# The first batch's chain: the bias row made earlier, VectorE by halves, identity products in TensorE's idle stretches

## The chip, the cores and the metric

The kernel runs on one core of a Trainium2 chip. The metric is device time in microseconds (us) for one launch of the whole program, here the median over runs. Before the change it is 997.85 us over 3 runs (994.13 to 998.16).

## What is computed

Two transformer layers over 8 sequences of 256 tokens, 256 features, in f32. Only the first attention matters here: every step that the change touches belongs to it, or to the bias table of the second attention that is built meanwhile.

```python
proj = x @ w_qkv                       # 2048 x 768
q, k, v = split(proj)                  # 16 heads of 16
q, k = apply_rope(q, cos, sin), apply_rope(k, cos, sin)
q = layernorm(q, ln_scale, ln_bias)    # over the 16 of a head
k = layernorm(k, ln_scale, ln_bias)
a = tril((q @ k.T) ** 4)
out = (a / sum(a)) @ v @ w_out
...
rel = clip(pos[None] - pos[:, None] + 63, 0, 126)
scores = scores + rel_pos[rel].mean(-1)    # second attention's bias
```

## The kernel before

Each engine has its program written out by hand, in order, and waits on semaphores. The layers are phases. Phase 0 and 1 (first attention and its feed-forward) run together over 8 batches of 256 tokens, each batch as 8 slots (two heads per slot); then comes the second attention, then the experts. f32 accuracy is kept by splitting an operand in a high and a low part and making three products (lines 445, 446 and 447, one helper).

Ahead of slot 0 of batch 0 stands a start that nothing overlaps with, and the change is in it alone. Its steps before the change:

- TensorE (PE): `x_turn(0, 0)` turns x (line 641). `qk(0, 0, t)`, six products of 512 columns for each token half t, waits for the first attention's weights. Between the two halves stands the product of line 870, which lays the means of the relative table out as a row; it waits for `rel_step`, counted by VectorE. Then `v(0, 0)` (12 products of 256 columns), `x_turn(0, 1)`, and the product of line 879, which mirrors the skewed bias and waits for two loads. Then `qk(0, 1, 0..1)` for batch 1, and `heads(0, 0, 0..1)` (line 676), which turn the first heads of batch 0 and wait for `split_ready`. Then the slots.
- VectorE (DVE): low parts of x and of the weights (lines 1694, 1754, 1954), the sum over the relative table and its scale (lines 1757 and 1759), then batch 0's chain: rotation of each token half (`rope_half`, lines 1786 to 1789, three operations), with the three copies of the bias row between them (`diagonal`, lines 1766 to 1768), rotated sum, sum per head, centring, scale, variance, reciprocal, normalising and bias over all 1024 columns at once (lines 1794 to 1823), the copy of the mirrored bias (line 1967) and eight low parts of the heads (line 1833). After them `rope_half(1, t)` of batch 1, and slot 0's fourth power (line 1842), which waits for GpSimd's masks.
- ScalarE (ACT): high parts, the square of the centred values (line 1286), the deviation (1291), eight high parts of heads (1302), the copies of turned heads (1247, 1307), then the squares of scores (1332).
- SyncE (SP): loads of x, weights, tables and the relative table (line 482), the first six tiles of the feed-forward's weights (line 487), then it waits for `diag_ready`, stores the bias row to memory (line 505), waits for it and loads it skewed (line 509).

Batch 0's `in_step` runs to 13, as each later batch's does.

## Time and profile before

| | |
|---|---|
| median of 3 runs | 997.85 us (994.13 to 998.16) |
| the profiled execution | 999.12 us, its span 997.1 us |
| PE busy | 882.9 us, 89% |
| DVE busy | 704.8 us, 71% |
| ACT busy | 693.2 us, 70% |
| POOL busy | 260.6 us, 26% |
| mean granted TensorE clock | 0.967 |

A row of the timeline has the start in us from the span's start, the time from the first to the last instruction that it merges, engine, line, operation, output and inputs, and in brackets the idle time of the engine ahead of it with what ended it. A matmul's duration is longer than the distance to the next, since they are pipelined: the price of one in a row of many is the distance between starts.

### The profile page before, as it was taken

The page shows a single profiled execution, that of the slowest core. Times are in us where ns is not written, and L with a number is a line of the kernel's source. Part 1 is how long each engine was busy: PE and PEld are TensorE (multiplying, and loading weights), DVE is VectorE, ACT ScalarE, POOL GpSimd, SP SyncE. Part 2 cuts the span into 40 slices and gives each one's busy share as a digit, 9 for nine tenths or more (in the row PEclk, how much of TensorE's full clock was granted, in tenths as well). Part 3 has the DMA queues.
Part 4 walks back from the last instruction along what each step waited for, and adds up shares of the span by engine and source line. Part 5 has one row for each costly group of instructions (what it writes and reads, how often), then busy time and mean ns, then how long its engine had stood idle before and what let it go on. Part 6 is the DMA issues. An engine that isn't in the chain of part 4 may idle for free.

```text
span 997.1 us, 21097 instructions
## 1 busy us (share of the span) xinstructions
PE 882.9 (89%) x7200; PEld 719.8 (72%) x7200; DVE 704.8 (71%) x2130; ACT 693.2 (70%) x1538; POOL 260.6 (26%) x360
## 2 busy tenths in 40 slices
PE   4778899999899988888989898989888999899995
PEld 3556788888788975666666666666665888789884
DVE  6877788888855567778787778787777562365437
ACT  2878766867765358988888888888888322366646
POOL 0345622333432202002020102010100347334432
PEclk9989999999999989999999999999999999999997
DMA  6203022010000102011111111101020312244434
GB/s 191 65 1 107 5 72 86 12 33 23 22 23 23 43 12 65 2 26 42 26 40 27 38 30 33 34 10 46 9 62 23 101 55 94 70 112 113 113 129 183
DMA packets 54761, 54.87 MB, mean 55 GB/s; under 512 B 17953, under 2 KB 48929, under 8 KB 54658
## 3 DMA queue, kind: packets, MB, share of 16 engines
q1 hardware_dynamic: 51250, 44.18, 15.1%
q0 software_dynamic: 3408, 9.34, 2.8%
q8 instruction: 61, 1.00, 0.4%
q14 instruction: 42, 0.34, 0.1%
HBM read 32.85 MB, written 20.65 MB: 54 GB/s over the span
## 4 chain that ended last, share of the span: by engine, by line
PE 53%; DVE 18%; ACT 16%; issue 8%; DMA 2%; POOL 1%; another core or an unknown queue 1%; DVEq 0%; ACTq 0%; SPq 0%; POOLq 0%
PE ps L445 11%; PE ps L447 10%; PE ps L446 10%; PE ps L968 5%; PE ps L985 4%; ACT G L1487 4%; PE ps L676 3%; PE ps L956 3%; ACT wu_rows L1487 3%; ACT G L1497 2%; DVE G L2032 2%; PE ps L749 2%; PE ps L1154 1%; ACT RT L1247 1%; DVE wu_rows L2032 1%
## 5 line engine op out<-in xcount | busy, mean ns | idle before, releaser
L1487 ACT ACTIVATE G<-G,small 128x256 f32<-128x256 f32 x296 | 133.3, 511 | 25.2 <-DVE small L2032 25.0
L2032 DVE CUSTOM_DVE_ANT_0 G<-ps,nb 128x256 f32<-128x256 f32 x296 | 111.2, 420 | 44.1 <-PE ps L956 43.7
L445 PE MATMUL ps<-WU 128*128 128x256 f32 x384 | 117.0, 305 | 17.1 <-DVE wu_rows L1854 6.9
L1497 ACT COPY G<-ps 128x512 f32<-128x512 f32 x192 | 112.1, 584 | 13.9 <-PE ps L968 13.5
L2393 POOL TENSOR_SCALAR_AFFINE_SELECT G<-G 128x256 f32<-128x256 f32 x128 | 76.4, 620 | 146.5 <-ACT G L1332 146.3
L446 PE MATMUL ps<-WU 128*128 128x256 f32 x384 | 108.4, 282 | 0.0
L447 PE MATMUL ps<-WU 128*128 128x256 f32 x384 | 108.3, 282 | 0.0
L1487 ACT ACTIVATE wu_rows<-wu_rows,small 128x256 f32<-128x256 f32 x216 | 97.7, 510 | 15.2 <-DVE small L2032 14.9
L2032 DVE CUSTOM_DVE_ANT_0 wu_rows<-ps,nb 128x256 f32<-128x256 f32 x216 | 81.3, 420 | 32.4 <-PE ps L956 32.1
L968 PE MATMUL ps<-ident,G 128*128 128x128 f32 x592 | 91.8, 283 | 13.3 <-DVE G L2042 9.5
L2360 POOL TENSOR_SCALAR small<-small 128x2 f32<-128x2 f32 x16 | 7.0, 440 | 324.6 <-DVE small L1678 324.6
L445 PEld LDWEIGHTS ps<-WU 128*128 128x128 f32 x384 | 72.8, 189 | 25.5 <-issue 9.3
L968 PEld LDWEIGHTS ps<-ident,G 128*128 128x128 f32 x592 | 65.8, 142 | 26.8 <-issue 8.2
L676 PE MATMUL ps<-ident,RT 128*128 128x128 f32 x512 | 72.3, 288 | 10.6 <-ACT RT L1247 7.3
L1332 ACT ACTIVATE G<-ps 128x768 f32<-128x768 f32 x64 | 52.3, 818 | 36.8 <-PE ps L732 32.9
L968 PE MATMUL ps<-ident,wu_rows 128*128 128x128 f32 x432 | 66.8, 282 | 10.3 <-DVE G L2042 9.1
L446 PEld LDWEIGHTS ps<-WU 128*128 128x128 f32 x384 | 73.2, 191 | 0.4
L956 PE MATMUL ps<-RT 32*128 32x256 f32 x512 | 64.7, 330 | 9.9 <-DVE small L2032 8.9
L985 PE MATMUL ps<-G 128*32 128x256 f32 x1024 | 68.5, 385 | 5.1 <-ACT G L1261 4.4
L447 PEld LDWEIGHTS ps<-WU 128*128 128x128 f32 x384 | 73.0, 190 | 0.0
L676 PEld LDWEIGHTS ps<-ident,RT 128*128 128x128 f32 x512 | 60.0, 147 | 17.9 <-ACT RT L1247 10.1
L956 PEld LDWEIGHTS ps<-RT 32*128 32x128 f32 x512 | 38.5, 184 | 46.6 <-issue 33.9
(251 smaller groups left out, 2374.4 us busy)
## 6 DMA issues: line engine op xcount, KB each, us to landing
xs<-G SPq DMA_DIRECT2D x8, 645.0 KB, 6.7
G<-xs SPq DMA_DIRECT2D x39, 128.0 KB
G<-x SPq DMA_DIRECT2D x17, 256.0 KB, 2.9
G<-in_x SPq DMA_DIRECT2D x16, 256.0 KB, 2.9
wu_rows<-yy SPq DMA_DIRECT2D x8, 512.0 KB, 6.9
x<-G SPq DMA_DIRECT2D x15, 256.0 KB, 2.2
wu_rows<-in_wu SPq DMA_DIRECT2D x8, 384.0 KB, 5.1
wraw<-in_wu SPq DMA_DIRECT2D x8, 256.0 KB, 3.0
```

The costliest lines, as they stand in the source:

```text
L445: pe.matmul(o, lh, rh, start=start, stop=False, skip_group_check=True)
L446: pe.matmul(o, lh, rl, start=False, stop=False, skip_group_check=True)
L447: return pe.matmul(o, ll, rh, start=False, stop=stop, skip_group_check=True)
L676: m = pe.transpose(ps[:, bank, S * g + P * t:S * g + P * (t + 1)], w[:, t, 2 * n + g, :], ident[:])
L956: m = pe.matmul(ps[:, SCORE_BANKS[n % 3], S * t:S * (t + 1)], QT[r, g, P * t:P * (t + 1)], KTT[r, g, :], start=True, stop=True, tile_posit ...
L968: m = pe.transpose(ps[:, 2 + h % 2, S * kt + P * t:S * kt + P * (t + 1)], prob(H2 * i + h)[:, t, P * kt:P * (kt + 1)], ident[:])
L985: m = pe.matmul(ps[32 * j:32 * j + 32, MIX_BANK, S * (quad % 2):S * (quad % 2 + 1)], vp[:, kt, at:at + 32], probT(h)[:, kt, :], start=kt = ...
L1332: act.square(U(p), ps[:, b:b + 2, 0:384]).then_inc(squared, 1)
L1487: m = act.activation(p, p, ACT.Exp, scale=-1.0, bias=mneg[:, k:k + 1])
L1497: act.copy(probT(h), halves(2 + h % 2)).then_inc(probT_act, 1)
L2032: m = dve.tensor_tensor_reduce(prob(H2 * i + h)[:, t, :], ps[:, SCORE_BANKS[h % 3], S * t:S * (t + 1)], nbv[:, t, :], 1.0, -FMIN, ALU.add, ...
L2393: m = pool.affine_select(out=u, in_=u, compare_op=ALU.is_ge, fill=0.0, base=0, pattern=[[0, 2], [1, P]], channel_multiplier=-1)
```

## The change

In `first_layer` of three engines, ahead of the slots:

- PE: the product that makes the bias row stands ahead of `qk(0, 0, 0)`. `keep_busy(n)` makes n plain f32 products of the identity with itself, 128 columns, in a bank that nothing reads then: 8 after the bias row's product, 30 after `x_turn(0, 1)`, 12 after the mirroring product and, after a wait for the first batch's variance (`in_step` 14), 6 more: 56 in all.
- VectorE: the sum over the relative table and its scale stand ahead of the weights' low parts, so the wait for that load does too. The three copies of the bias row are gone from it. Each token half is rotated, summed and centred by itself; scale, variance and reciprocal stay whole; normalising and bias go by halves of the heads, each followed by its four low parts, with the copy of the mirrored bias in the first half.
- ScalarE: makes the three copies of the bias row, after the weights' high parts; the centred squares go by token halves; the high parts of each half of the heads wait for that half alone.

Batch 0 now has 19 steps in `in_step`, and `in_at(b, s)` finds a batch's step. The later batches' work is unchanged.

```diff
@@ -862,21 +867,31 @@
+                def keep_busy(times):
+                    for _ in range(times):
+                        pe.matmul(ps[:, MIX0, 0:P], ident[:], ident[:], start=True, stop=True)
                 x_turn(0, 0)
+                pe.wait_ge(rel_step, 2)
+                pe.matmul(ps[0:1, 0, 0:TABLE], small[0:TABLE, 16:17], ident[0:TABLE, 0:TABLE],
+                          start=True, stop=True).then_inc(diag_row, 1)
+                keep_busy(8)
                 pe.wait_ge(xt_ready[0], 1)
                 pe.wait_ge(aw0_ready, 2)
                 qk(0, 0, 0)
-                pe.wait_ge(rel_step, 2)
-                pe.matmul(ps[0:1, 0, 0:TABLE], small[0:TABLE, 16:17], ident[0:TABLE, 0:TABLE],
-                          start=True, stop=True).then_inc(diag_row, 1)
                 qk(0, 0, 1)
                 pe.wait_ge(aw0_ready, 3)
                 v(0, 0)
                 x_turn(0, 1)
+                keep_busy(30)
                 pe.wait_ge(skewed, 32)
                 pe.wait_ge(flip_ready, 2)
                 pe.matmul(ps[:, 1, :], flip, skewed_bias, start=True, stop=True).then_inc(bias_turned, 1)
+                keep_busy(12)
+                pe.wait_ge(in_step, in_at(0, 14))
+                keep_busy(6)
                 pe.wait_ge(xt_ready[0], 2)
                 for t in range(2):
                     qk(0, 1, t)
@@ -1281,20 +1296,34 @@
+                def diagonal():
+                    act.wait_ge(diag_row, 1)
...
+                def first_squares(t):
+                    act.wait_ge(in_step, in_at(0, 6 + 6 * t))
+                    act.square(SQ[:, 512 * t:512 * (t + 1)], CEN[:, 512 * t:512 * (t + 1)]).then_inc(cen_squared, 1)
...
                 def head_hi_parts(b):
-                    act.wait_ge(in_step, IN_STEPS * b + 13)
                     for g in range(2):
+                        act.wait_ge(in_step, in_at(b, 13 if b else 17 + 2 * g))
...
+                diagonal()
                 stage_v(0, 0)
-                centred_squares(0)
+                first_squares(0)
                 x_hi(0, 1)
+                first_squares(1)
@@ -1749,25 +1780,15 @@
                 x_lo(0, 0)
-                for k in range(KT):
-                    dve.wait_ge(aw0_hi, k + 1)
-                    dve.tensor_tensor(AW[:, 1, k, 0:512], aw0_in[:, k, 0:512], AW[:, 0, k, 0:512].bitcast(F32), ALU.subtract
-                                      ).then_inc(aw0_ready, 1)
                 dve.wait_ge(rel_loaded, 16)
                 dve.tensor_reduce(small[0:TABLE, 15:16], small[0:TABLE, 0:D2], AX_X, ALU.add).then_inc(rel_step, 1)
...
+                for k in range(KT):
+                    dve.wait_ge(aw0_hi, k + 1)
...
+                def first_centred(t):
+                    of, groups = slice(512 * t, 512 * (t + 1)), slice(2 * H0 * t, 2 * H0 * (t + 1))
+                    dve.wait_ge(in_step, in_at(0, 3 + 6 * t))
+                    step(in_step, in_at(0, 4 + 6 * t), dve.tensor_tensor(ROT[:, of], ROT[:, of], ROT2[:, of], ALU.add))
+                    step(in_step, in_at(0, 5 + 6 * t), dve.tensor_reduce(hsum[:, groups], rh[:, groups], AX_X, ALU.add))
...
+                def first_normalised(g):
...
+                    step(in_step, in_at(0, 16 + 2 * g), dve.tensor_tensor(r, r, by, ALU.mult))
+                    dve.tensor_tensor(s, r, lnt[:, D0:2 * D0].unsqueeze(1).unsqueeze(1).to_broadcast(part), ALU.add).then_inc(in_step, 1)
@@ -1953,19 +2004,17 @@
-                rope_half(0, 0)
-                diagonal()
-                rope_half(0, 1)
-                rotated(0)
-                centre(0)
-                times_scale(0)
-                variance(0)
+                for t in range(2):
+                    rope_half(0, t)
+                    first_centred(t)
+                first_scaled()
                 x_lo(0, 1)
-                normalised(0)
-                plus_bias(0)
-                dve.wait_ge(bias_turned, 1)
-                dve.tensor_copy(nb[:], ps[:, 1, :]).then_inc(bias_ready, 1)
+                first_inverse()
                 for g in range(2):
+                    first_normalised(g)
+                    if g == 0:
+                        dve.wait_ge(bias_turned, 1)
+                        dve.tensor_copy(nb[:], ps[:, 1, :]).then_inc(bias_ready, 1)
                     lo_parts(0, g)
```

`first_scaled` is the scale and the variance over all 1024 columns as before, and `first_inverse` the reciprocal.

TensorE's order ahead of the first slot, before. Line 641 is `x_turn`, 870 the bias row's product, 879 the mirroring one, 676 `heads`; rows of lines 445 to 447 are the products of `qk` and `v`.

```order
L641 MATMUL ps<-ident,G 128x128 x3
L445 MATMUL ps<-AW,RT 128x512 [waits aw0_ready,xt_ready0]
...
L447 MATMUL ps<-AW,RT 128x512
L870 MATMUL ps<-ident,small 1x127 [waits rel_step]
L445 MATMUL ps<-AW,RT 128x512
...
L641 MATMUL ps<-ident,G 128x128 [waits xt_loaded0]
L641 MATMUL ps<-ident,G 128x128 x3
L879 MATMUL ps<-G 128x512 [waits flip_ready,skewed]
L445 MATMUL ps<-AW,RT 128x512 [waits xt_ready0]
...
L676 MATMUL ps<-ident,RT 128x128 [waits split_ready0]
```

And with the change (646 is `x_turn`, 877 the bias row's product, 873 an identity product, 891 the mirroring one, 681 `heads`):

```order
L646 MATMUL ps<-ident,G 128x128 x3
L877 MATMUL ps<-ident,small 1x127 [waits rel_step]
L873 MATMUL ps<-ident 128x128 x8
L450 MATMUL ps<-AW,RT 128x512 [waits aw0_ready,xt_ready0]
...
L646 MATMUL ps<-ident,G 128x128 x3
L873 MATMUL ps<-ident 128x128 x30
L891 MATMUL ps<-G 128x512 [waits flip_ready,skewed]
L873 MATMUL ps<-ident 128x128 x12
L873 MATMUL ps<-ident 128x128 [waits in_step]
L873 MATMUL ps<-ident 128x128 x5
L450 MATMUL ps<-AW,RT 128x512 [waits xt_ready0]
...
L681 MATMUL ps<-ident,RT 128x128 [waits split_ready0]
```

Ahead of the first q and k product there now stand the bias row's product, with its wait, and 8 identity products; 48 more stand between `x_turn(0, 1)` and the first `heads`, on the one queue of the engine.

VectorE's order from the low parts of x to the first low parts of the heads, with the change (1816, 1817 and 1819 are the rotated sum, the sum per head and the centring; 1839 and 1840 normalising and bias; 1884 a low part):

```order
L1725 TENSOR_TENSOR RT<-ps,RT 128x512 [waits xt_hi0]
L1784 TENSOR_REDUCE small<-small 127x1 [waits rel_loaded]
L1786 TENSOR_SCALAR small<-small 127x1 [waits rel_step]
L1790 TENSOR_TENSOR AW<-G,AW 128x512 [waits aw0_hi] x2
...
L1816 TENSOR_TENSOR G<-G 128x512 [waits in_step]
L1817 TENSOR_REDUCE small<-G 128x32 [waits in_step]
L1819 SCALAR_TENSOR_TENSOR G<-small,G 128x512 [waits in_step]
...
L1839 TENSOR_TENSOR G<-G,small 128x4x128 [waits in_step]
L1840 TENSOR_TENSOR G<-G,lnt 128x4x128 [waits in_step]
L2017 COPY nb<-ps 128x512 [waits bias_turned]
L1884 TENSOR_TENSOR RT<-G,RT 128x2x8x16 [waits split_hi0]
```

The two small operations moved ahead of the weights' low parts, three operations of 1024 columns became six of 512 and two became four, and the first low parts stand behind half of the normalising.

## Rows read from the trace of the kernel before

**Rows 1.** Timeline of TensorE, the start (start, time, engine, line, operation):

```profile
3.65 1.09 PE L641 MATMUL ps<-ident,G 128*128 128x128 f32 x4 [3.65 <-DMA G<-in_x]
8.79 0.77 PE L445 MATMUL ps<-AW,RT 128*128 128x512 f32 x1 [4.05 <-DVE AW L1754]
...
11.61 0.58 PE L870 MATMUL ps<-ident,small 127*1 127x127 f32 x2
12.13 0.80 PE L445 MATMUL ps<-AW,RT 128*128 128x512 f32 x1
...
15.82 0.60 PE L641 MATMUL ps<-ident,G 128*128 128x128 f32 x4
```

**Rows 2.** The chain that ended last, in order of time, 10 to 34 us:

```profile
10.40 0.43 PE ps L445
...
13.82 3.29 DMA ediag<-G
17.50 4.16 DMA G<-ediag
21.70 2.07 PE ps L879 x2
...
27.85 0.23 PE ps L446
28.08 0.23 PE ps L447
28.31 0.45 PE ps L676 x4
...
32.78 0.96 DVE ring L1842
```

**Rows 3.** Timeline of VectorE, the start:

```profile
8.55 0.16 DVE L1757 TENSOR_REDUCE small<-small 127x1 f32<-127x8 f32 x1
8.74 0.15 DVE L1759 TENSOR_SCALAR small<-small 127x1 f32<-127x1 f32 x1
11.72 0.69 DVE L1786 TENSOR_TENSOR G<-ps,ropet 128x512 f32<-128x512 f32 x1 [1.31 <-PE ps L447]
12.99 0.27 DVE L1766 COPY G<-ps 1x127 f32<-1x127 f32 x1
14.59 0.69 DVE L1786 TENSOR_TENSOR G<-ps,ropet 128x512 f32<-128x512 f32 x1 [0.81 <-PE ps L447]
15.98 1.22 DVE L1794 TENSOR_TENSOR G<-G 128x1024 f32<-128x1024 f32 x1
17.24 1.22 DVE L1795 TENSOR_REDUCE small<-G 128x64 f32<-128x1024 f32 x1
26.58 2.77 DVE L1833 TENSOR_TENSOR RT<-G,RT 128x256 fp32r<-128x256 f32 x8
29.39 0.69 DVE L1786 TENSOR_TENSOR G<-ps,ropet 128x512 f32<-128x512 f32 x1
32.78 0.96 DVE L1842 TENSOR_TENSOR ring<-G 128x768 f32<-128x768 f32 x1 [0.78 <-POOL G L2393]
```

**Rows 4.** Timeline of TensorE at the experts, plain f32 products of 128 columns at full clock:

```profile
809.13 0.38 PE L1122 MATMUL ps<-G,nb 128*128 128x128 f32 x2
809.35 0.39 PE L1123 MATMUL ps<-G,nb 128*128 128x128 f32 x2
```

**Rows 5.** Timeline of SyncE's queue, the loads around the relative table's:

```profile
3.90 0.30 SPq L482 DMA_DIRECT2D small<-in_rel  x1
8.93 2.01 SPq L487 DMA_DIRECT2D wu_rows<-in_wu  x4
```

**Rows 6.** The loads of x, line 475: from issue to landing:

```profile
DMA to landing us min/median/max: 2.7/2.7/2.7
```

**Rows 7.** Stretches (from:to, length, busy PE, PEld, DVE, ACT, POOL, granted clock, DMA share, GB/s):

```profile
22.00:24.00 2.00, 2.00 (x4) 0.82 (x4) 1.97 (x4) 0.35 (x1) 0.00 (x0) 0.50 0.00 0
45.00:50.00 5.00, 1.47 (x19) 0.99 (x20) 3.80 (x9) 4.28 (x11) 0.79 (x2) 0.80 0.27 72
50.00:55.00 5.00, 5.00 (x20) 4.20 (x20) 2.87 (x7) 2.74 (x5) 1.76 (x2) 0.52 0.00 0
55.00:60.00 5.00, 3.49 (x40) 2.46 (x39) 3.79 (x6) 3.33 (x6) 2.40 (x4) 1.00 0.01 3
```

More of the change, by code:

```diff
@@ L406, in raw_count, with in_at @@
             return 16 * sum(dmas(n) for n in range(load + 1))
+        def in_at(b, s):
+            return FIRST_STEPS + IN_STEPS * (b - 1) + s if b else s
         def on_act(h):
@@ new lines, in first_scaled, with first_inverse @@
+                def first_scaled():
+                    step(in_step, in_at(0, 13), dve.tensor_tensor(rh, ch, lnt[:, 0:D0].unsqueeze(1).to_broadcast(full), ALU.mult))
+                    dve.wait_ge(cen_squared, 2)
+                    dve.tensor_reduce(hvar, sh, AX_X, ALU.add).then_inc(in_step, 1)
+                def first_inverse():
+                    dve.wait_ge(head_std, 1)
+                    step(in_step, in_at(0, 15), dve.reciprocal(hrs, hrs))
+                def first_normalised(g):
+                    part = [P, 4, H0 // 2, D0]
+                    of = slice(H0 // 2 * g, H0 // 2 * (g + 1))
+                    r, s = (a.rearrange("p (n h d) -> p n h d", n=4, h=H0)[:, :, of] for a in (ROT, SQ))
+                    by = hrs.rearrange("p (n h) -> p n h", n=4)[:, :, of].unsqueeze(3).to_broadcast(part)
+                    step(in_step, in_at(0, 16 + 2 * g), dve.tensor_tensor(r, r, by, ALU.mult))
+                    dve.tensor_tensor(s, r, lnt[:, D0:2 * D0].unsqueeze(1).unsqueeze(1).to_broadcast(part), ALU.add).then_inc(in_step, 1)
```

48 lines of the change are left out of this document (26 added, 22 removed).

## The prediction

> **What bounds the kernel now.** I read the page first: TensorE is busy 89% of the span, VectorE 71%, ScalarE 70%. But the change touches the first 30 us alone, where nothing overlaps with batch 0's chain, so I went on to the timelines of the start and to the chain that ended last. A microsecond won before the first slot is worth one at the end at most, and so is one lost.
>
> TensorE has three stretches of work in the start [rows 1]. It turns x, waits 4.05 us for the weights, makes q, k and v from 8.79 on, and turns x again at 15.82. At first 512 columns take 0.43 us each; near the end of such a series it is 0.23 us [rows 2]: the first figure is the engine at 1.2 GHz, the second at 2.4 GHz. It then idles until the skewed bias has landed at 21.66 (17.50 + 4.16), makes the mirroring product and batch 1's q and k, mostly at the low clock, and starts turning the heads at 28.31 [rows 2].
>
> VectorE meanwhile runs batch 0's chain nearly without a gap: it starts when the first six products end (11.72) and ends at 29.35 (26.58 + 2.77), that is 17.6 us later [rows 3]. Half of its low parts, those which the heads wait for, are out at about 28.0, 16.3 us after 11.72. So two chains meet at 28.0 to 28.3: VectorE's low parts and TensorE's products. From the heads to the first fourth power at 32.78 are 4.47 us [rows 2], and VectorE waited 0.78 us for it, having ended batch 1's rotation at 32.0 [rows 3]. The rest of the kernel follows from there.
>
> **The part ahead of the first q and k product.** The identity products cost TensorE time, since its queue is in order. At full clock a plain f32 product of 128 columns is two matmuls, and the next starts 0.22 us later (809.13 to 809.35) [rows 4]. At half clock I take double, 0.44 us; the bias row's product, of 127 columns, took 0.52 with its neighbour's wait (11.61 to 12.13) [rows 1]. These are the two ends.
>
> When can they start? Not before the sum over the relative table. Its load is issued at 3.90 [rows 5]; its landing isn't in the trace. No earlier than 6.6, with the 2.7 us of the quickest load, that of x [rows 6]; no later than 8.55, when VectorE did the sum with no idle time before it [rows 3]. I take 8.0, nearer the row that is on this very data. The two small operations need 0.35 us (8.55 to 8.90), so TensorE starts at 8.35. Product 0.5, eight identities 8 x 0.44 = 3.5: q and k can start at 12.4. The weights' low parts, moved behind the load (8.35 + 2 x 0.65 = 9.65), are ready by then and cost nothing; without the identities they would cost 0.9.
>
> On this load the Trainium skill has a rule (DMA: Bandwidth & Descriptors, "Why a DMA increments its semaphore by 16 and not by 1"): a transfer of 127 partitions runs on a single one of the 16 DMA engines. That speaks against a quick landing, and by it I would take the late end, 8.55: the sum would be 0.5 us higher. The trace shows neither.
>
> The clock: the fast spacing came at 13.9, 5.1 us after TensorE took up work at 8.79, and in the second series at 27.6, 5.9 us after 21.70. From 8.35 the nearer value gives 13.5. So two and a half of the six products go at 0.43 and the others at 0.23, with 0.2 for the last one's end: 12.4 + 1.1 + 0.8 + 0.2 = 14.5. VectorE's chain starts at 14.5 in place of 11.72, **2.8 us late**. Ends: landing at 6.6 gives 13.0, landing at 8.55 with the clock 5.9 us later gives 15.4.
>
> **VectorE's chain.** 1024 columns are 1.22 us and 1.26 from start to start (15.98 to 17.24), 512 are 0.69, so about 0.72 in a dependent series [rows 3]. Rotation 1.35, centred half 3 x 0.72 = 2.16, and again: 7.0. Scale and variance 2.52: 9.5; low part of x and reciprocal: 10.75. First half of the heads 2 x 0.72, the bias copy 0.65, four low parts 1.4: 14.25. Second half 1.45 and 1.4: 17.1. The three copies gone from VectorE (0.8 from 12.99 on) and the idle 0.81 at 14.59 pay for halving. So it is 2.0 us shorter to the first heads (14.25 against 16.3) and 0.5 to the end. ScalarE's copies lie where it idles, its squares beside VectorE's scale, its high parts one ahead of VectorE's low ones: nothing. By this chain the heads could be turned at 28.75 and batch 1's rotation (2.7 us) ends at 34.3.
>
> **TensorE's queue behind it.** From 14.3: second q and k half 6 x 0.227 = 1.4, v 12 x 0.12 = 1.4, x turned 0.6: 17.7. Thirty identities, now at full clock, 6.6: 24.3. The skewed bias has long landed, so its wait is gone: the store of the row is issued some 2.9 us earlier (10.94 in place of 13.82, behind six weight tiles whose last issue ends at 8.93 + 2.01) [rows 2, 5], but whether it lands earlier does not matter. Mirroring product at full clock 0.9 (2.07 at half): 25.2. Twelve identities 2.6: 27.8. The variance was there at 24.0; six more 1.3: 29.1. Batch 1's q and k 12 x 0.227 = 2.7: **31.8**. The heads then stand at 31.9 in place of 28.31, 3.6 us late, and VectorE's low parts wait for TensorE, not the reverse. First fourth power: 31.9 + 4.47 = 36.4 in place of 32.78. Batch 1's rotation (34.3) is no longer what pair 1's scores wait for, so something is given back in the first slots; I take 0.4.
>
> **Sum.** 3.6 - 0.4 = +3.2 us: 999.12 becomes 1002.3. That execution lay 1.3 us above the median of the runs, so I forecast a median of **1001.0 us**. With the ends of the landing and the clock the cost is 2.0 to 4.5.
>
> About 0.5% (5.0 us, so 992.9 and 1002.8) is what a measurement of this kernel can tell from no change; the three runs alone spread over 4.0.
>
> **Rivals.**
> - *Identities are cheap (chance 0.14).* If one in a row of many costs less than 0.156 us, the 48 fit in the 7.5 us between TensorE's other work (21.3) and the low parts at 28.75. Against it are rows 4 with 0.22. Then VectorE decides: rotation ends at 34.3 in place of 32.78 for the fourth power, +1.5 us, so 999.3. The Trainium skill (TensorE: Matmul & The Clock Gate, "Back-to-back issue gap") gives about 81 ns for a matmul of 128 columns in a stream with weight loads, so 0.16 us for the two; by that it would be on the border of this case. Rows 4 show 0.11 each.
> - *The clock pays it back, not slower than before (0.20).* Right after the start, at 45 to 50, TensorE is busy 1.47 of 5 us, and then, at 50 to 55, busy all of the time at a granted 0.52, at 2.87 for VectorE [rows 7]. That low stretch is on the path. With TensorE's own idle time filled in the start and batch 1's products done ahead of slot 0, the gap at 45 may shrink enough that the clock stays up. Price: 5.0 us at half clock are 2.5 won, with the neighbouring edges 3.4. 3.2 - 3.4 = -0.2: 997.7. It decides the result if the granted clock stays at 1.00 over the 10 us from 45 on (from 48 on, with the shift). For it: TensorE without a pause in the start stays at full clock (it was 0.50 at 22 to 24 [rows 7]). Against: the work of the slots, which makes that gap, is the same.
> - *The start is wholly cold (0.16).* The table lands at 8.55 and the clock rises only behind the first q and k: the chain starts at 15.4, heads +4.5. A further low stretch of the length of the one at 50 to 55 then falls in the first slots and adds 3.4: +7.9, 1005.7.
> - *Forecast (0.50)*: 1000 to 1003.
>
> **How the numbers follow.** Faster by over 0.5% needs the second rival and a start at its early end, and 3 us more: 0.04. Slower by over 0.5% is the third rival with the upper edge of the forecast: 0.18. The rest, 0.78, is within 0.5%. The range 995.0 to 1004.5 takes in the forecast with its ends, the first rival and most of the second; a tenth is left out at each side.
>
> **What would show it.** In the changed profile: the relative table's sum at 8.0 to 8.6; the first q and k product at 12 to 13 and not at 8.8; VectorE's first rotation at 13.0 to 15.4; identity products 0.22 apart, 0.44 before the clock rises; the granted clock at 1.00 from 14 to 35; no wait ahead of the mirroring product; the first heads at 31 to 33 with TensorE busy before them, and VectorE idle some 2 us ahead of its first fourth power. I am wrong if the identities end before VectorE's low parts, or if the first fourth power comes at the old time or sooner, or if the low clock at 50 to 55 is gone.

## The result and the profile after

The changed kernel takes 1003.94 us (median of 5 runs, 1003.65 to 1006.11), the kernel before in runs beside it 996.76 (5 runs, 994.13 to 998.16). The ratio is 1.0080 [1.0062, 1.0098]: slower by 0.8%. The forecast was 1001.0; the time lies inside the range of 995.0 to 1004.5, close to its upper end, but slower by over 0.5% had been given a chance of 0.18 only. A later comparison of the same two kernels gave 1.0079 [1.0054, 1.0104].

| | before | after |
|---|---|---|
| the profiled execution | 999.12 us, span 997.1 | 1003.65 us, span 1001.6 |
| PE busy | 882.9 us | 891.4 us |
| DVE busy | 704.8 us | 705.9 us |
| ACT busy | 693.2 us | 694.5 us |
| mean granted TensorE clock | 0.967 | 0.973 |

TensorE is 8.5 us busier, in matmuls that nobody reads, and its mean clock is higher; the time is longer. Where it came from is in the first 40 us. TensorE's timeline of the changed kernel (columns as in [rows 1]):

```profile
8.85 0.58 PE L877 MATMUL ps<-ident,small 127*1 127x127 f32 x2 [4.05 <-DVE small L1786]
9.36 3.78 PE L873 MATMUL ps<-ident 128*128 128x128 f32 x16
12.79 0.77 PE L450 MATMUL ps<-AW,RT 128*128 128x512 f32 x1
...
15.04 0.39 PE L452 MATMUL ps<-AW,RT 128*128 128x512 f32 x1
15.27 0.40 PE L450 MATMUL ps<-AW,RT 128*128 128x512 f32 x1
...
18.52 6.86 PE L873 MATMUL ps<-ident 128*128 128x128 f32 x60
25.23 1.02 PE L891 MATMUL ps<-G 128*128 128x512 f32 x2
26.09 4.18 PE L873 MATMUL ps<-ident 128*128 128x128 f32 x36
30.02 0.48 PE L450 MATMUL ps<-AW,RT 128*128 128x512 f32 x1
...
32.87 1.03 PE L681 MATMUL ps<-ident,RT 128*128 128x128 f32 x8
```

The first q and k product stands at 12.79 where it was at 8.79 [rows 1]. Ahead of it are the wait for the relative table (to 8.85) and eight identity products, 3.43 us from 9.36 to 12.79. From 15.04 to 15.27 the spacing is 0.23: the clock is up from there. From 12.79 to 35 TensorE has no gap over 0.3 us: the 60 matmuls of the thirty identity products take 6.71 us, the 36 of the later eighteen 3.93, and batch 1's products and the heads wait their turn behind them. The heads start at 32.87, where they started at 28.14 by the same timeline (the chain of [rows 2], which goes by ends, has 28.31).

VectorE's timeline of the changed kernel:

```profile
8.44 0.16 DVE L1784 TENSOR_REDUCE small<-small 127x1 f32<-127x8 f32 x1 [2.30 <-DMA small<-in_rel]
...
15.47 0.69 DVE L1807 TENSOR_TENSOR G<-ps,ropet 128x512 f32<-128x512 f32 x1 [4.35 <-PE ps L452]
...
28.36 1.43 DVE L1884 TENSOR_TENSOR RT<-G,RT 128x256 fp32r<-128x256 f32 x4 [0.18 <-ACT RT L1331]
...
31.89 1.43 DVE L1884 TENSOR_TENSOR RT<-G,RT 128x256 fp32r<-128x256 f32 x4 [0.78 <-ACT RT L1331]
33.36 0.69 DVE L1807 TENSOR_TENSOR G<-ps,ropet 128x512 f32<-128x512 f32 x1
...
37.51 1.13 DVE L1893 TENSOR_TENSOR ring<-G 128x768 f32<-128x768 f32 x1 [1.53 <-POOL G L2442]
```

The table's sum is done at 8.44 after 2.30 us of waiting for the load, so it landed 4.5 us after its issue at 3.90. The chain starts at 15.47 in place of 11.72 [rows 3], its first four low parts are out at 29.8, ahead of the heads at 32.87, and the first fourth power is at 37.51 in place of 32.78: 4.7 us later. The chain of waits of the changed kernel says the same from behind (start, length, what held):

```profile
3.90 4.51 DMA small<-in_rel
8.85 0.58 PE ps L877 x2
9.43 3.71 PE ps L873 x16
...
18.69 6.70 PE ps L873 x60
...
26.25 4.02 PE ps L873 x36
...
37.51 1.13 DVE ring L1893
```

All 56 identity products stand on it, 14.4 us: what was meant to fill idle time is now on the critical path.

SyncE's queue in the changed kernel shows what the early bias row bought:

```profile
11.70 0.29 SPq L510 DMA_DIRECT2D ediag<-G  x1
17.67 0.80 SPq L514 DMA_DIRECT2D G<-ediag  x2
```

The store is issued 2.1 us earlier than at 13.82 [rows 2], but SyncE waits for it until 17.67, before until 17.11 (13.82 + 3.29). That is 6.0 us after its issue, behind the six weight tiles issued ahead of it. The Trainium skill (DMA: Bandwidth & Descriptors, "Queues, rings and completion order") has each DMA engine take the descriptors of one queue in ring order. A late store behind six tiles would fit that, but no run here takes the tiles away, so the cause is not shown.

And the stretches of the changed kernel that answer to [rows 7] (busy us of PE, PEld, DVE, ACT and POOL, granted clock, DMA share, GB/s):

```profile
22.00:24.00 2.00, 2.00 (x21) 2.00 (x20) 1.93 (x3) 0.63 (x1) 0.00 (x0) 1.00 0.18 60
45.00:50.00 5.00, 4.49 (x32) 2.84 (x28) 4.11 (x5) 3.38 (x7) 2.36 (x4) 0.66 0.81 254
50.00:55.00 5.00, 1.88 (x22) 1.12 (x22) 3.38 (x8) 4.37 (x11) 0.79 (x2) 0.75 0.26 66
55.00:60.00 5.00, 5.00 (x21) 4.28 (x22) 3.19 (x8) 2.65 (x5) 2.18 (x2) 0.56 0.00 0
```

The clock is at full speed at 22 to 24, as meant. But the low stretch of the first slots has only moved: TensorE is busy 5.00 of 5 us at a granted 0.56 from 55 on. Nothing is paid back: the fifth fourth power is at 62.51, before at 57.53, so 5.0 us late.

### The profile page after: what moved, and what is told of

It reads as the page before. It is cut to its first block, busy times and chain, and to the rows that moved or that the text cites. A ratio compares the mean times of both kernels' runs of the same rounds, so it can differ in the third digit from the quotient of the medians.

```text
span 1001.6 us, 21327 instructions
## 1 busy us (share of the span) xinstructions
PE 891.4 (89%) x7312; PEld 730.3 (73%) x7312; DVE 705.9 (70%) x2132; ACT 694.5 (69%) x1542; POOL 261.8 (26%) x360
## 4 chain that ended last, share of the span: by engine, by line
PE 56%; DVE 18%; ACT 14%; issue 8%; DMA 1%; POOL 1%; SPq 0%; DVEq 0%; ACTq 0%; POOLq 0%
PE ps L450 11%; PE ps L452 10%; PE ps L451 10%; PE ps L983 5%; PE ps L1000 5%; ACT G L1518 4%; PE ps L681 3%; PE ps L971 3%; ACT wu_rows L1518 3%; DVE G L2081 2%; ACT G L1528 2%; PE ps L873 1%; PE ps L754 1%; PE ps L1169 1%; ACT RT L1262 1%
## 5 line engine op out<-in xcount | busy, mean ns | idle before, releaser
L1518 ACT ACTIVATE G<-G,small 128x256 f32<-128x256 f32 x296 | 133.4, 511 | 26.1 <-DVE small L2081 26.0
L2081 DVE CUSTOM_DVE_ANT_0 wu_rows<-ps,nb 128x256 f32<-128x256 f32 x216 | 81.2, 419 | 31.8 <-PE ps L971 31.5
L1361 ACT ACTIVATE G<-ps 128x768 f32<-128x768 f32 x64 | 52.2, 816 | 37.3 <-PE ps L737 32.9
```

What stands on the lines that cost most here:

```text
L1361: act.square(U(p), ps[:, b:b + 2, 0:384]).then_inc(squared, 1)
L1518: m = act.activation(p, p, ACT.Exp, scale=-1.0, bias=mneg[:, k:k + 1])
L2081: m = dve.tensor_tensor_reduce(prob(H2 * i + h)[:, t, :], ps[:, SCORE_BANKS[h % 3], S * t:S * (t + 1)], nbv[:, t, :], 1.0, -FMIN, ALU.add, ...
```

## Experiments

The theory behind all of them: every identity product costs its full time on TensorE's in-order queue. The rivals: that the table's early wait is the cost, that the chain by halves is (ScalarE's part of it had been taken as nothing), or that the loss lies in later stretches of low clock. Measured milestones are put together in a table at the end of this section.

### First set: one part at a time

Kernel a, no identity products at all:

```diff
-                keep_busy(8)
-                keep_busy(30)
-                keep_busy(12)
-                pe.wait_ge(in_step, in_at(0, 14))
-                keep_busy(6)
```

> The change without any of the 56 identity products; all else as changed. Theory A (TensorE's own queue makes the delay, the identity products fill it and the start's delay goes to the end one for one): the first q and k product at 10.1, VectorE's chain starts at 12.9 (changed kernel 15.5, before 11.7), TensorE idles again ahead of the mirroring product until the skewed bias lands at about 22, heads at 28.5, first fourth power at 33.0 (changed kernel 37.5, before 32.8). Time within 1 us of before, 997. Theory R (the work by halves, the moved wait for the table or the ScalarE copies cost the time): heads stay at 31 or later, time 1001 or more. Theory C (the low clock stretches behind the start differ, and that is the loss): heads at 28.5, but the time stays over 1000.

Measured: ratio 1.0027 [1.0000, 1.0053]. Of the 0.8%, 0.5 are gone. A third seems to be left without a single identity product, but the interval reaches down to none. TensorE's timeline of this kernel:

```profile
27.82 1.03 PE L681 MATMUL ps<-ident,RT 128*128 128x128 f32 x8
30.20 1.15 PE L681 MATMUL ps<-ident,RT 128*128 128x128 f32 x8 [1.34 <-ACT RT L1258]
```

The first heads are at 27.82, within what the kernel before shows (28.1, 27.3 and 26.7 in three profiles), although the chain starts 0.9 to 2.0 us later, at 12.66. But the second pair of heads waits 1.34 us for ScalarE's copy of the first, where it waited 0.24 before, and the first fourth power comes at 33.56, later than in any of those three.

Kernel b, only the first eight taken out:

```diff
-                keep_busy(8)
```

> The change without the 8 identity products ahead of the first q and k product; the other 48 stay. Theory A: VectorE's chain starts at 12.9, but TensorE's queue sets the heads: x turned at 17.3, 30 products of 0.22 to 24.0, mirroring to 24.9, 18 more to 28.9, batch 1's q and k to 31.6. Heads at 31.6, 1.4 earlier than changed; time 1.4 us below the changed kernel, 1002.5. If VectorE's chain were the limit: heads 2.6 us earlier than changed, time 1001.3.

Measured: 1.0063 [1.0029, 1.0097], the first fourth power at 34.94, 2.6 us sooner than in the changed profile above. Of the 3.4 us of queue, 2.8 are gone from the start of the chain (12.68 in place of 15.47); the clock rises at 13.0, behind the first q and k. The time shows 1.7 us, with 3.4 us of uncertainty either way in this ratio and 1.8 in the changed kernel's: that the first eight cost time is read from the trace, not from the times.

Kernel c, only the first eight left in:

```diff
-                keep_busy(30)
-                keep_busy(12)
-                pe.wait_ge(in_step, in_at(0, 14))
-                keep_busy(6)
```

> The change with the first 8 identity products alone; the 48 behind x_turn are out. Theory A: VectorE's chain starts at 15.5 as changed, and it is the limit now: low parts at 29.8, heads at 29.8 (TensorE's products are done by 29), batch 1's rotation ends at 36.0 and the first fourth power comes at 36.0 in place of 37.5. Time 1.5 us below the changed kernel, 1002.4. So each group taken out alone gives 1.4, both together 4.5. If the 48 were hidden behind VectorE's chain: the same time as changed.

Measured: 1.0043 [1.0014, 1.0072], first fourth power at 35.79. TensorE's timeline of this kernel:

```profile
22.43 2.08 PE L890 MATMUL ps<-G 128*128 128x512 f32 x2 [4.33 <-DMA G<-ediag]
25.23 0.77 PE L450 MATMUL ps<-AW,RT 128*128 128x512 f32 x1 [0.71 <-DVE RT L1722]
...
30.48 1.46 PE L681 MATMUL ps<-ident,RT 128*128 128x128 f32 x8
```

The chain starts at 14.89 with the eight and at 12.66 without any (a), and the heads that stand at 30.48 here stand at 32.87 with the 48. So in the traces both groups cost; the intervals of the times overlap. Without the later 48 the engine idles for 4.33 us, the clock falls, and batch 1's twelve products take 5.25 us (25.23 to 30.48) where they take 2.85 at full clock (30.02 to 32.87 in the changed kernel). The filling does what it is meant to do, worth 2.4 us, and costs 48 x 0.22 = 10.6 against a wait of 4.3 to 6.5 (4.33 here, 5.10 to 6.52 in the profiles of the kernel before).

Kernel d, the kernel before with the chain by halves alone (bias row, its copies on VectorE, table sum where they were; no identity product):

```diff
-                rope_half(0, 0)
-                diagonal()
-                rope_half(0, 1)
-                rotated(0)
-                centre(0)
-                times_scale(0)
-                variance(0)
+                rope_half(0, 0)
+                diagonal()
+                first_centred(0)
+                rope_half(0, 1)
+                first_centred(1)
+                first_scaled()
```

> Before, with VectorE's chain and ScalarE's part of it by halves alone: bias row's product, its copies on VectorE and the sum over the table where they were, no identity products. Theory A: the low parts of the first heads come at 26.8 in place of 28.0, but TensorE is at the mirroring product until 21.7 and at batch 1's products, at the low clock, until 28.3 as before: heads 28.3, first fourth power at 32.8, time as before within 0.5 us (996.8). Theory R (halving costs more in fixed shares than it gives): the fourth power at 33.5 or later and the time up by 1 or more.

Measured: 1.0012 [0.9995, 1.0030]: no gain. TensorE's timeline of this kernel:

```profile
27.70 1.03 PE L681 MATMUL ps<-ident,RT 128*128 128x128 f32 x8
29.82 1.14 PE L681 MATMUL ps<-ident,RT 128*128 128x128 f32 x8 [1.09 <-ACT RT L1258]
```

The same wait again, 1.09 us. VectorE's part from the first rotation to batch 1's is 18.48 us here, and 17.67 in the kernel before [rows 3]: halving makes it longer.

### Second set: a pure delay, the table, and filling in other places

Kernel e, the kernel before with 24 identity products directly ahead of the first heads:

```diff
+                keep_busy(24)
                 heads(0, 0, 0)
```

> Before, with 24 identity products directly ahead of the first heads and nothing else: a pure delay of 24 x 0.22 = 5.3 us on TensorE's queue. Theory A (a delay of the first heads goes to the end one for one): heads at 33.4, first fourth power at 38.0, time +5.2 (996.8 to 998.6 becomes 1002 to 1004). Theory C (the clock's low stretches behind the start decide): the first fourth power 5.2 later, and the time higher by another amount, 2 to 9.

Measured: 1.0049 [1.0029, 1.0070]. TensorE's timeline of this kernel:

```profile
29.17 5.52 PE L868 MATMUL ps<-ident 128*128 128x128 f32 x48
34.52 1.04 PE L676 MATMUL ps<-ident,RT 128*128 128x128 f32 x8
```

The 24 delay the heads by 5.35 us (29.17 to 34.52); the time is longer by 4.9, with an interval of 2.9 to 7.0. A delay at this place is paid about one for one, as far as this interval tells; no later slack takes it up. (The profiled execution, 1004.23 us, is the slowest of its seven; its first fourth power, 39.16, is 7.2 us behind the mean of the kernel before, since its chain also started late, at 12.45.)

Kernel f, the changed kernel with the table's load moved up to stand behind that of x:

```diff
+            sp.dma_start(small[0:TABLE, 0:D2], rel).then_inc(rel_loaded, 16)
...
-            sp.dma_start(small[0:TABLE, 0:D2], rel).then_inc(rel_loaded, 16)
```

> The changed kernel with the load of the relative table issued right behind the load of x, ahead of the weights' two loads. Theory A (the wait for the table holds up the first q and k product, together with the 8 identities behind it): the table's sum at about 5 to 6 in place of 8.44, identities end at about 10 in place of 13, VectorE's chain starts at 11.5 to 12.5 in place of 15.5, heads at about 29.5 in place of 33.0. Time 3 to 4 us below the changed kernel, 1000. If the table's wait is nothing: time as changed, 1004.

Measured: 1.0022 [1.0002, 1.0041]. VectorE's timeline of this kernel:

```profile
6.10 0.15 DVE L1784 TENSOR_REDUCE small<-small 127x1 f32<-127x8 f32 x1
...
11.86 0.68 DVE L1807 TENSOR_TENSOR G<-ps,ropet 128x512 f32<-128x512 f32 x1
...
33.75 0.96 DVE L1893 TENSOR_TENSOR ring<-G 128x768 f32<-128x768 f32 x1 [1.39 <-POOL G L2442]
```

The sum now runs at 6.10 with no wait, and the first fourth power is 3.8 us sooner than in the changed profile above. So one line of SyncE's queue wins back most of the loss: what made the first eight dear is that they stand behind a wait that ends late. Even then the changed kernel does not reach the old start (11.86 and 33.75; 10.68 to 11.72 and 31.36 to 32.78 before). Its twelve times fall in two groups of six, 995.8 to 998.3 and 1001.4 to 1004.0, for which no cause is shown; the profiled one is of the upper, and the median lies between them.

Kernel g, halves, with the copies of the bias row on ScalarE and the bias row, table sum and weights' low parts in the old order; 8 identity products directly behind `x_turn(0, 0)`, where TensorE waits for weights, 30 behind `x_turn(0, 1)`, none later:

```diff
                 x_turn(0, 0)
-                pe.wait_ge(rel_step, 2)
-                pe.matmul(ps[0:1, 0, 0:TABLE], small[0:TABLE, 16:17], ident[0:TABLE, 0:TABLE],
-                          start=True, stop=True).then_inc(diag_row, 1)
                 keep_busy(8)
...
-                keep_busy(12)
-                pe.wait_ge(in_step, in_at(0, 14))
-                keep_busy(6)
```

> The work by halves and the bias row's copies on ScalarE as changed, but the bias row's product, the sum over the table and the weights' low parts in the order of before; 8 identity products directly behind the first x_turn, in the 4 us in which TensorE waits for the weights, and 30 behind the second x_turn, in the wait for the skewed bias; none after it. Theory A: first q and k product at 8.8 and at full clock from about 9 to 10 on, VectorE's chain starts at 10.3 to 10.8 (before 11.7); the 30 identities end at 20.7, ahead of the landing at 21.9; batch 1's products end at 25.5 at full clock; first fourth power at 30.9 (before 32.8). Time 1.9 us below before. Theory R (halves cost more than they give): fourth power at 32 or later.

Measured: 1.0027 [1.0009, 1.0045]. ScalarE's timeline of this kernel:

```profile
27.61 1.32 ACT L1328 CAST RT<-G 128x256 fp32r<-128x256 f32 x4 [2.21 <-DVE G L1837]
28.84 0.57 ACT L1259 CAST RT<-ps 128x512 fp32r<-128x512 f32 x1
...
30.26 0.58 ACT L1259 CAST RT<-ps 128x512 fp32r<-128x512 f32 x1 [0.36 <-PE ps L681]
```

Here the cause of the new wait is plain. The first heads are turned from 26.30 on, but ScalarE's copies of them (line 1259) stand in its queue behind the high parts of the second half (line 1328), which wait 2.21 us for VectorE. They run at 28.84, and the second pair of heads, which waits 2.07 us for them, at 29.46. Heads that are early on TensorE are held on ScalarE.

Kernel h, the same filling with the chain left whole, that is, the kernel before with 8 and 30 identity products and the copies of the bias row on ScalarE:

```diff
                 x_turn(0, 0)
+                keep_busy(8)
...
                 x_turn(0, 1)
+                keep_busy(30)
```

> Before, with the bias row's copies on ScalarE and the 8 and 30 identity products placed as in g_fill_halves; VectorE's chain whole, not by halves. Theory A: chain starts at 10.3 to 10.8, low parts of the first heads 15.4 later at 26.0, end of the chain 16.8 later at 27.3, batch 1's rotation ends at 30.0, heads at 26.0, first fourth power at 30.5. Time 2.2 us below before; the same as g within 0.5, since halving helps the heads and costs VectorE.

Measured: 0.9971 [0.9959, 0.9983]. TensorE's timeline of this kernel:

```profile
4.64 3.62 PE L868 MATMUL ps<-ident 128*128 128x128 f32 x16
8.41 0.76 PE L445 MATMUL ps<-AW,RT 128*128 128x512 f32 x1
...
21.90 1.12 PE L886 MATMUL ps<-G 128*128 128x512 f32 x2 [0.27 <-DMA G<-ediag]
...
26.08 1.09 PE L676 MATMUL ps<-ident,RT 128*128 128x128 f32 x8 [0.31 <-DVE RT L1841]
```

The eight end at about 8.3, and the first q and k product follows at 8.41, within what the kernel before shows (8.79, 7.74, 7.75 in three profiles); the thirty end 0.27 us ahead of the bias's landing; the heads wait for VectorE. The first fourth power is at 30.77 and, in a second profile, at 30.01. VectorE's part is 16.68 us long: 1.0 us shorter than before for the three copies that went to ScalarE, 1.2 shorter than the 17.89 by halves.

### Third set: ScalarE's order, an earlier start, a cheaper product

Kernel i, as g, with ScalarE's copies of the turned heads between the two halves of its high parts:

```diff
-                head_hi_parts(0)
                 for q in range(2):
+                    head_hi_parts(0, [q])
                     turned_heads(0, q)
```

> g_fill_halves with ScalarE's copies of the first turned heads between its high parts of the first and of the second half of the heads, in place of behind both. Theory H (the first half is out early, but the copies of the turned heads wait behind the second half's high parts on ScalarE's in-order queue, so halving can't help the heads): first copies at 26.9 in place of 28.84, second turning of heads at 28.0 in place of 29.46, first squares of scores at 29.5 to 30 in place of 31.7; VectorE's second low parts 0.4 later; the first fourth power is then set by VectorE's own chain, at 32.8 in place of 33.4. Time 0.5 below g, so 998 to 1000. Theory K (the copies are not what it waits for): squares stay at 31.7.

Measured: 1.0045 [1.0029, 1.0061]. ScalarE's timeline of this kernel:

```profile
26.53 0.59 ACT L1259 CAST RT<-ps 128x512 fp32r<-128x512 f32 x1 [2.63 <-PE ps L681]
...
27.49 1.33 ACT L1328 CAST RT<-G 128x256 fp32r<-128x256 f32 x4
...
29.68 0.84 ACT L1358 ACTIVATE G<-ps 128x768 f32<-128x768 f32 x1
33.12 0.81 ACT L1358 ACTIVATE G<-ps 128x768 f32<-128x768 f32 x1 [2.60 <-PE ps L737]
```

And VectorE's second low parts:

```profile
28.25 1.43 DVE L1881 TENSOR_TENSOR RT<-G,RT 128x256 fp32r<-128x256 f32 x4 [1.56 <-ACT RT L1328]
```

The copies run at 26.53 instead of 28.84 and the squares of pair 0 at 29.68 instead of 31.75: the place of the wait is shown. But no time is won: the first fourth power, at 32.24, still stands behind VectorE's part, and pair 1's squares wait 2.60 us. The new order has moved the wait to the other side. ScalarE's second high parts now stand behind the copies, so VectorE waits 1.56 us for them where it waited 0.78 in g, and its part is 19.28 us long (10.43 to 29.71) in place of 17.89. One in-order queue serves both VectorE and the heads, and in each of the two orders tried one of them waits.

Kernel j, as h, with four identity products more ahead of `x_turn(0, 0)`:

```diff
+                keep_busy(4)
                 x_turn(0, 0)
                 keep_busy(8)
```

> h_fill_whole with 4 more identity products ahead of the first x_turn, while x is being loaded (1.5 to 3.7). Theory A (TensorE's work before raises the clock sooner): full clock by 8 to 9 in place of 9.8, chain starts at 10.2 to 10.5 in place of 10.72, first fourth power 0.2 to 0.6 earlier; time as h_fill_whole within 0.6, so 994.5, some 3 below before. Rival: the 4 hold up the turning of x: it starts later than 3.8 and the weights' first low part is waited for no more; then up to 0.3 slower than h.

Measured: 1.0006 [0.9987, 1.0025], although this profile's first fourth power, at 29.75, is the earliest so far. A start that is some 2 us earlier is not seen in the time; the table below shows where the profiles lose it again.

Kernel k, the changed kernel with a transpose, one matmul, in place of the f32 product, which is two:

```diff
-                        pe.matmul(ps[:, MIX0, 0:P], ident[:], ident[:], start=True, stop=True)
+                        pe.transpose(ps[:, MIX0, 0:P], ident[:], ident[:])
```

> The changed kernel with each of the 56 identity products made as a transpose: one matmul in place of two, so 0.11 to 0.12 us at full clock in place of 0.22, and 0.22 in place of 0.43 at half. Theory A (the queue time of the identity products is the cost): the first eight end at 11.2 in place of 12.8, VectorE's chain starts at 14.0, the 48 end 5.3 us earlier relative to the turning of x, TensorE waits for the skewed bias or the variance, and VectorE's chain (17.9 to batch 1's rotation) sets the first fourth power at about 34.8 in place of 37.5. Time 2 to 3 us below the changed kernel. If transposes did not hold the clock up: granted clock 0.5 before 25 us and the products of batch 1 spaced 0.43, the heads at 31 or later.

Measured: 1.0029 [1.0011, 1.0046]. TensorE's timeline of this kernel:

```profile
8.86 1.97 PE L873 MATMUL ps<-ident 128*128 128x128 f32 x8
...
17.00 3.44 PE L873 MATMUL ps<-ident 128*128 128x128 f32 x30
21.58 1.12 PE L891 MATMUL ps<-G 128*128 128x512 f32 x2 [1.14 <-DMA G<-ediag]
22.54 2.13 PE L873 MATMUL ps<-ident 128*128 128x128 f32 x18
...
27.80 1.09 PE L681 MATMUL ps<-ident,RT 128*128 128x128 f32 x8 [0.37 <-DVE RT L1884]
30.96 1.60 PE L681 MATMUL ps<-ident,RT 128*128 128x128 f32 x8 [2.07 <-ACT RT L1262]
```

At half the price the products fit: the mirroring product waits for its data, the heads wait for VectorE, and 5 us of the loss are gone. This is the first rival of the prediction, made true, which gave it +1.5 us; measured are 2.9, with an interval of 1.1 to 4.6. The wait of the second heads for ScalarE, 2.07 us, is back with it: in the changed kernel, where the identity products hold the first heads back to 32.87, it is 0.24.

The changed kernel once more, in the same set:

> The changed kernel once more beside before, for a closer ratio. Theory A (all of the loss is the late start, 4.7 us at the first fourth power): ratio 1.0047, time 1002.5 where before is 997.9. Theory M (the 7.2 us between the medians are real, and 2.5 us of them arise behind the start): ratio 1.007 or more.

Measured: 1.0079 [1.0054, 1.0104], its first fourth power at 36.25 (1.3 us sooner than in the first profile of it, since the clock rose at 12.5 and not at 15.0).

### Fourth and fifth set: again, and the spread between executions

h and j once more, and two further profiles each of the kernel before and of the changed one, one of each at a time.

> h_fill_whole again, beside j_again on one chip. Theory A: first fourth power about 2 us ahead of before, ratio 0.997 to 0.998. Theory N (the gain of h was chance, the first batches' low clock stretches spread it): ratio over 0.999.

Measured: 0.9998 [0.9983, 1.0014].

> j_warm_earlier again, beside h_again on one chip. Theory A: first fourth power about 3 us ahead of before, ratio 0.996 to 0.998 and not above h's. Theory P (an earlier start pays back what it won behind it, in the stretches of low clock): ratio 1.000 or more, above h's, with a fourth power at 30 and a rest of 941 us or more.

Measured: 1.0004 [0.9988, 1.0021].

> The kernel before, one more trace. The start should vary little: first fourth power at 31.5 to 33.5. Theory S: from there to the end 963 to 965. Theory M: 961 to 963, shorter than the changed kernel's rest.

> The changed kernel, one more trace. Theory S (the missing 3 us lie in the start): first fourth power at 38 to 41, more than 5 us behind before's. Theory M (behind it): first fourth power at 36 to 38, and from there to the end 965 us or more (before 964.3).

> The kernel before, one more trace. First fourth power at 31.5 to 33.5. Theory S: from there to the end 963 to 965. Theory M: 961 to 963.

> The changed kernel, one more trace. Theory S: first fourth power at 38 to 41. Theory M: at 36 to 38, and from there to the end 965 us or more.

These four single executions took 996.48 and 1005.64, 994.55 and 1002.00 us. h's gain of 0.3% did not come back: it beats the changed kernel in both sets, but that it beats the kernel before is not shown. All profiles together, in us:

| kernel | chain starts | heads | first fourth power | fifth | ratio |
|---|---|---|---|---|---|
| before, three profiles | 11.72, 10.68, 10.69 | 28.1, 27.3, 26.7 | 32.8, 32.0, 31.4 | 57.5, 56.8, 55.6 | 1 |
| changed, four profiles | 15.47, 14.22, 14.09, 14.61 | 32.9, 31.6, 31.5, 32.0 | 37.5, 36.3, 36.1, 36.7 | 62.5, 60.7, 60.6, 61.1 | 1.0080, 1.0079 |
| a, no identities | 12.66 | 27.8 | 33.6 | 60.5 | 1.0027 |
| b, without the first 8 | 12.68 | 30.3 | 34.9 | 60.2 | 1.0063 |
| c, the first 8 only | 14.89 | 30.5 | 35.8 | 61.3 | 1.0043 |
| d, halves only | 11.70 | 27.7 | 33.2 | 59.3 | 1.0012 |
| e, delay of 5.35 | 12.45 | 34.5 | 39.2 | 64.4 | 1.0049 |
| f, table first | 11.86 | 29.1 | 33.8 | 58.1 | 1.0022 |
| g, filled, halves | 11.93 | 26.3 | 33.4 | 59.6 | 1.0027 |
| i, g with copies between | 10.43 | 25.9 | 32.2 | 58.5 | 1.0045 |
| k, transposes | 13.43 | 27.8 | 34.9 | 61.1 | 1.0029 |
| h, filled, whole | 10.72, 9.94 | 26.1, 25.3 | 30.8, 30.0 | 56.6, 54.5 | 0.9971, 0.9998 |
| j, as h, 4 more | 10.32, 9.32 | 25.1, 24.7 | 29.8, 29.4 | 54.4, 53.5 | 1.0006, 1.0004 |

Three profiles of the kernel before put its first fourth power at 32.0 on average, four of the changed one at 36.6. The start costs 4.6 us, and the fifth fourth power (56.6 and 61.2) still shows 4.6. Behind the first fourth power the spans have 964.3, 962.4 and 961.1 us left before, and 964.1, 963.5, 967.6 and 963.4 after: 2.0 more on average. The longest of them, 967.6, has a stretch of low clock of 13.7 us at 374, where the other three have one of 6.8; which executions get one could not be tied to the change.

The traces do show where most of the 2.0 arise. GpSimd's cast into WU (128x384) near the end of the second attention is at 762.48, 761.87 and 758.68 before, and at 767.32, 763.82, 768.22 and 763.90 in the changed kernel: 4.8 apart on average, so up to there hardly anything is added to the start's 4.6. From it to the end of the span are 234.6, 232.5 and 233.8 us before and 234.3, 235.9, 235.5 and 236.1 after, 1.8 more. The work there is the same, and over all 20 profiles this stretch is 232.5 to 236.3 us long, so its cause stays open: seven profiles can't tell an effect of the change from the spread between executions. The same stretch has the kernel j at 236.3 and 236.0, 2.5 over the mean of the kernel before. Its first fourth power is early by as much (29.75 and 29.40 against 32.0); its spans, 995.4 and 992.3, are hardly shorter than 997.1, 994.4 and 992.5.

## Why the prediction was wrong

**In the start the mechanism held.** Identity products at full price in front of the first q and k and of the heads, a late chain, nothing waited for at the mirroring product, heads held by TensorE and not by VectorE, VectorE idle ahead of its first fourth power: all of it is in the trace. The price of one, 0.22 us at full clock and 0.44 at half, is measured as 0.224 (60 matmuls in 6.71 us) and 0.43 (16 in 3.43). The delay of 24 products shows that what the start loses is lost at the end, within its interval of 2.9 to 7.0 us for 5.35. The step that failed is what comes behind the start; two smaller ones are the base and the sizes.

**"The rest of the kernel follows from there" and "something is given back in the first slots; I take 0.4": the step that failed.** The sum takes 0.4 us off for all that comes behind the first fourth power. Nothing is given back: the changed kernel is 4.7 late at the first fourth power and 5.0 at the fifth in the first pair of profiles, 4.6 and 4.6 over all. And the rest does not just follow: over all profiles it is 2.0 us longer than before, 1.8 of them behind 762 us, mostly in the experts' time. Of the 4.0 us between the forecast difference of 3.2 and the measured one of 7.2 between the medians, 3.0 lie here: the 0.4, and 2.6 more. Why that last part takes longer is not shown.

**The part ahead of the first q and k: off by 1.0 us in the first profile.** The forecast takes the landing at 8.0, "nearer the row that is on this very data". The table landed at 8.42, near the end that the prediction kept as bound: q and k at 12.79 and not at 12.4. The larger piece is the clock: "from 8.35 the nearer value gives 13.5" became 15.0, so that five of the first six products went at 0.43. The chain began at 15.47, 0.07 beyond the latest end of 13.0 to 15.4. In the other three profiles of the changed kernel the rise came at 12.5 to 12.9 and the chain at 14.1 to 14.6, about the forecast 14.5. There the table's sum ran at 8.05 to 8.66 and not at 8.0, and the clock rose 0.6 to 1.0 us ahead of the forecast 13.5. The two misses work against each other: that the forecast fits so well is in part luck. The range is not added up right either: with the chain at 13.0 and 15.4 and the 0.4 taken off, the cost is 1.7 to 4.1 and not 2.0 to 4.5.

**TensorE's queue behind it: right.** It carried the 1.0 us through: 25.23 (24.3), 26.09 (25.2), 30.02 (29.1), heads 32.87 (31.9), first fourth power 37.51 (36.4). Over the four profiles the first fourth power is at 36.6 on average: the start of the changed kernel was forecast to 0.2 us on average.

**"ScalarE's copies ..., its high parts one ahead of VectorE's low ones: nothing": wrong, and hidden.** The first half came as forecast: low parts out 14.3 us after the start (14.25). The end did not: 17.9 and not 17.1, since VectorE waits 0.18 and 0.78 us for ScalarE's high parts ([rows 3] have the whole form, without). And ScalarE's copies of the heads queue behind the second half's high parts, so that the second heads wait 1.1 to 2.1 us in the kernels a, d, g and k. In the changed kernel the heads come so late that neither holds them up. So the halves gain nothing even where TensorE is not late: by themselves they measure 1.0012 [0.9995, 1.0030].

**The base of the sum, "First fourth power: ... in place of 32.78": 0.8 us too late.** The sum was made against a profile whose start was the latest of three (32.78, the others 31.97 and 31.36), and then taken 1.3 us down to the median as if that execution's extra were elsewhere. 0.8 us of it are in the start itself, in the very number that the loss was counted from: against the mean of 32.0 the loss there is 4.6 and not 3.6. So of a difference of medians of 7.2 us, where 3.2 were forecast, 0.8 are the base, 0.2 the sizes, 0.4 the give-back that did not come, and 2.6 what the rest adds. The chances had a like fault: 1002.8 was the bound for "slower", the forecast was 1001.0 with its own bounds at 1000 and 1003, and a spread between executions of 4 us, which the prediction had named, was not put into them. And a third rival at 1005.7 with a chance of 0.16 lies above the range's end of 1004.5, where only a tenth was said to be left out.

**The rivals.** Cheap identities: fell (0.224 each); made true in k, its mechanism held (the heads wait for VectorE), and its +1.5 us became 2.9. The clock pays it back: fell, the low stretch at 50 to 55 is at 52.5 to 59.4 now. Wholly cold start: its start came nearly true in the first profile (15.47, heads +4.7), its further low stretch in the first slots only in part: a short one at 45 to 50 (0.66). Its 1005.7 is 1.8 above the median.

## What to carry to other kernels

Filler on an in-order engine is free only while the engine waits for something that does not itself stand behind the filler, and only as long as count times price stays below that wait: the eight products cost 3.4 us behind the table's late wait and next to nothing directly behind the turning of x, where the same engine waited for weights. Work out the sum for each idle stretch from the trace: 48 x 0.22 = 10.6 us were put where 4 to 6 were idle, to win 2.4.

A chain cut in halves gains only if each engine that serves it can serve the halves in that order; look in its queue for what stands behind the second half's wait, and for who waits when you turn the order round. And take two or three profiles of the kernel before as base: starts here differ by 1.4 us between executions of the same program, nearly a third of the 4.6 us under study.

## What the runs showed of the hardware

- **The clock's rise is not at a fixed time in the program.** It came at 13.8, 13.2 and 11.3 us in three executions of the kernel before, at 15.0, 12.5, 12.5 and 12.9 in four of the changed one, at 9.8 and 7.0 in two of h and at 7.2 and 5.6 in two of j, in which TensorE hardly pauses before the first q and k. More work early brings it forward; within one kernel it still varies by up to 2.8 us (h).
- **Filling the start moves the later low stretch, it doesn't remove it.** In every profile of these kernels a stretch at about half clock begins between 44.6 and 55.1. In a, d, g, i, k and one of h there is another that begins between 29.9 and 33.3, where the work of the first heads is, and in one of j at 39.7. The two profiles of h, one with such a stretch and one without, have the first and fifth fourth power 25.8 and 24.5 us apart.
- **Transposes hold the clock up.** With TensorE idle for 5 us ahead of the mirroring product the clock fell [rows 7]; with 30 transposes there it did not. Stretches of the kernel k:

```profile
16.00:20.00 4.00, 4.00 (x39) 4.00 (x38) 3.83 (x8) 1.59 (x3) 0.00 (x0) 1.00 0.49 81
20.00:24.00 4.00, 2.87 (x21) 2.10 (x19) 3.93 (x5) 0.98 (x2) 0.00 (x0) 1.00 0.28 74
```

  The granted clock is 1.00 in both. The Trainium skill (TensorE: Matmul & The Clock Gate, "Part 4: PE-mode transpose") says that the full clock doesn't engage for transposes in this mode. The measurement goes against it here: a stream of `transpose` calls kept full clock, at half the queue time of the f32 product. Whether transposes alone would raise the clock is not shown.
- **A small load behind large ones is slow to land.** The table's, 127 partitions of 32 bytes (4 KB), took 4.5 us, the far larger one of x, first in the queue, 2.7 [rows 6]. The two loads issued just ahead of the table's, of 128 partitions of 128 bytes each, took 5.2 and 5.0 us in the same profile. And in the two further profiles of the kernel before, VectorE sums the table at 7.51 and 7.52, at most 3.6 us after its issue at 3.91. So its place behind the weights' loads may be all of it, and these rows don't bear out the Trainium skill's rule on 127 partitions (DMA: Bandwidth & Descriptors, "Why a DMA increments its semaphore by 16 and not by 1"), which the prediction quotes; nor do they refute it.
